# One pool of eight PSUM banks for attention and front, and a new written order of the steps

## The chip, the cores and the metric

The kernel runs on one core of a Trainium2 chip. The core has five engines that run their own instruction queues and meet only at semaphores: TensorE (PE: matmuls; its weight loads are listed as PEld), VectorE (DVE), ScalarE (ACT), GpSimd (POOL) and SyncE (SP, which issues most DMAs). Matmuls write to PSUM, eight banks of 128 partitions x 512 float32; DVE and ACT read the results from there. The metric is the device time of one execution in microseconds (us).

## The reference

The input is x, 8 batches of 512 tokens with 256 features, all in float32. With H = 16 heads of width 16 and a latent width of 32:

```
qkv = x @ c_attn_w.T + c_attn_b                 # q, k, v: 16 heads x 16
q_lat = q @ q2l_w.T + q2l_b; k_lat, v_lat with kv2l
q_lat, k_lat = rope(q_lat), rope(k_lat)         # t*cos + rotate_half(t)*sin
att = softmax(causal((q_lat @ wqk_w.T + wqk_b) @ k_lat.T * 32**-0.5))
y = (att @ v_lat) @ l2o_w.T + l2o_b;  x = layernorm(x + y @ cproj_w.T + cproj_b)
xn = layernorm(x)*g + b                         # as 4 x 1024 tokens
logits = xn @ (layernorm(slot_embeds)).T        # 16 experts x 64 slots
slots = softmax(logits over tokens).T @ xn      # dispatch
eout = (gelu(slots@Wg+bg) * (slots@Wu+bu)) @ Wd + bd    # F = 512, per expert
x = layernorm(x + softmax(logits over slots) @ eout)    # combine
```

The result has to agree with float32, so products that need it are done as three products of split operands (a high part of reduced precision and the rest).

## The kernel before

**Stages.** Setup (0 to 37 us) prepares weights. Attention (to about 558) works on one group of four heads at a time; a batch has four groups, written here as batch.group. The front of the second half (dispatch and the slots) overlaps attention's end and runs to 805; then come the sixteen experts (gate_up and the way down) and combine.

**Steps.** PE's work in attention and front is a list of named steps. In attention, for each group: `lat` (latent q and k), `wqk`, six `max` steps (scores of one shape each, line 1460, with the causal mask added by L1463), `neg` (transposes the negated row maxima, L1468), six `exp` steps (the scores again, transposed, with the maxima folded in, L1476), four `pv` steps (L1487) and `yT` (L1494). Once a batch: `v`, `yTT` (L1500), `cproj` (L1509). In the front, per round: `s1` (logits; split products, L455 to L457), `topT` (L1534), `topB` (L1540), `c2` (transposes of the combine weights, L1563), `sumT` (L1546), `sumB` (L1553), `zT` (L1516), `slots` (L455 to L457).

The other engines have lists of their own. DVE: `max` (reduces a max step, L1170), `negmax` (two instructions, L1178 and L1180), `qlo` (drains wqk's bank and makes the low part of q, L1164), `shuffle` (L1144), `cos` (L1160), `wv` (L1118 to L1121), `v`, `yT`, `ln` (the layernorm), `sel`, `slots` (L1277), `sumT` (L1267), `weight` (splits of expert weights, L1068 and L1071). ACT: `lat` (L817), `khi`, `qhi` (L845, L851), `exp` (drains an exp step with the exponential, L873), `y` (L880), `e` (L943, L944), `c2` (L962), `weight`. POOL: `sin` (L703), `add` (L709), `klo` (L713), `mask` (zeroes the part above the diagonal of the exponentials, L723; `pv` waits for it), `bias` (L729), `lo` (L740), `sum` (L745, L747). SP: `stack` (copies of q and k into the stacked layout that the score matmuls read, L410), `store`, `z`, `c2`, `slots` (L575), `weight` (L513; wg, wu, wd of an expert).

**Order.** Each list is made by `order()` (L55 to L95). A step of attention stands at 32 x batch + 8 x group + an offset in slots from tables such as `PE_AT` and `DVE_AT`; the first steps have places of their own in `PE_EARLY` and the like. The list is sorted by that. The front's steps come from lists for one round (`PE_FRONT`, and `PE_LAST` for the last), and `PE_JOIN` says how many attention steps are left when each of the first front steps comes in.

**PSUM.** `fills()` (L98 to L112) hands out three pairs of banks (`ring`) in turn to every step of `PAIR_STEPS`. The fourth pair (`tail`) is split: one bank, `misc`, for `wqk`, `neg` and `yT`, and one, `ybank`, for `pv`; it becomes a fourth pair behind the last of those. A PE step waits on one semaphore for its pair (or bank) to be drained:

```
    for n, s in enumerate(steps):
        if n == last:
            free.insert(0, RING)
        if s[0] in PAIR_STEPS:
            r = free.pop(0)
            free.append(r)
```

So a step waits for the third last holder of a pair, whichever that was. In a steady group, exp and max steps alternate, and the second `max` step of the next group has the pair of an `exp` step three back.

Of the kernel before, what the change touches and what calls it, by code (L numbers as in the profile page):

```python
# [38 lines left out]
UNIT_SLOTS = GROUP_SLOTS / len(MAX_UNITS)  # L39


PE_AT = {"lat": -20.25, "wqk": -9.25, "max": 0.0, "neg": 11.0, "exp": 13.25, "v": 14.55, "pv": 15.75, "yT": 28.75, "yTT": 53.5, "cproj": 58.5, "wv": -10.384, "seT": 5.624}
ACT_AT = {"stack": -9.0, "xth": -30.5, "lat": -22.0, "khi": -12.85, "qhi": -9.6, "neg": 9.57, "exp": 11.74, "y": 22.25, "yTT": 52.85, "apply": 76.25, "wlat": -30.402, "senorm": -2.024, "seT": 7, "seh": 9.429}
DVE_AT = {"xtl": -32.0, "blat": -28.9, "kvrows": -28.8, "slotg": -28.781, "shuffle": -21.3, "cos": -17.25, "qlo": -10.0, "max": -3.11, "negmax": 6.05, "v": 11.5, "yT": 26.15, "cproj": 55.1, "ln": 56.75, "wlat": -30.314, "wv": -17.071, "sestat": -23.24, "sescale": -7.5, "sel": 9.985}
POOL_AT = {"sin": -26.06, "add": -23.69, "klo": -21.92, "mask": 2.69, "bias": 42.5}
SP_AT = {"xt": -52.5, "x": 28.5, "stack": -22.15, "store": 83.25}

PE_EARLY = {("lat", 0, 1): -11.099, ("lat", 0, 2): -6.473, ("lat", 0, 3): 2.93, ("wqk", 0, 0): -9.817, ("wqk", 0, 1): -5.784, ("wqk", 0, 2): 5.42, ("v", 0): 14.309}
ACT_EARLY = {("lat", 0, 1): -17.39, ("lat", 0, 2): -6.025, ("lat", 0, 3): 2.059, ("khi", 0, 0): -14.377, ("khi", 0, 1): -5.841, ("khi", 0, 2): 5.453, ("qhi", 0, 0): -13.3, ("qhi", 0, 1): -4.402, ("qhi", 0, 2): 4.692, ("xth", 1): 1.5, ("stack", 0, 0): -6.105}
# [8 lines left out]

# [1640 lines left out]
```

## Time and profile before

| what | us |
|---|---|
| three runs | 1200.65, 1199.85, 1196.84; median 1199.85 |
| profiled execution | 1196.4, its span 1194.7 |
| busy in the span | PE 1140.9 (96%), DVE 780.1, ACT 662.9, POOL 579.2 |
| TensorE clock granted | 0.986 of full speed |

The span is the time from the first to the last instruction of the profiled execution. A busy share is the time in which an engine worked on something; PE's includes modelled ends of its pipelined matmuls, so that short pauses between them are not seen in it. The shares are means over stages that differ much, so the rows below are mostly of single stretches.

### The profile page before, as it was taken

The numbers are of one execution on the slowest core, as the hardware profiler recorded it, in microseconds if no ns is written. First come the engines' busy times: TensorE is split into PE (matmuls) and PEld (weight loads), VectorE is DVE, ScalarE is ACT, GpSimd is POOL, SyncE is SP. The second block draws the span as 40 slices with busy tenths as digits, with TensorE's granted clock in tenths as the row PEclk, the third lists the DMA queues.
The fourth block names the chain that finished last, engine by engine and source line by source line (L and its number), as shares of the span: only waits on it lengthen the run. The fifth ranks groups of instructions, "written<-read, shape, count | busy, mean of one in ns | idle before, by whom it ended". The sixth has DMA issues, their size and how long they took to land.

```text
span 1194.7 us, 19111 instructions
## 1 busy us (share of the span) xinstructions
PE 1140.9 (96%) x6849; PEld 897.2 (75%) x6882; DVE 780.1 (65%) x1251; ACT 662.9 (55%) x946; POOL 579.2 (48%) x399
## 2 busy tenths in 40 slices
PE   7799999999999999988999999979999999999996
PEld 5566667676666666656788888858888888888885
DVE  6878787979797978766677777644455454523344
ACT  2555466565656565656797777755555555530112
POOL 5555555555555556522666666664444544430000
PEclk9899999999999999999899999999999999999998
DMA  5645544645565454631144335365555445365661
GB/s 152 143 106 130 123 115 103 159 113 152 125 155 131 115 157 92 180 98 54 40 160 161 125 125 186 108 195 185 166 183 184 140 157 165 114 216 166 244 224 53
DMA packets 126670, 170.29 MB, mean 143 GB/s; under 512 B 47041, under 2 KB 77186, under 8 KB 126594
## 3 DMA queue, kind: packets, MB, share of 16 engines
q1 hardware_dynamic: 124018, 167.95, 48.2%
q10 hardware_dynamic: 2576, 1.35, 0.5%
q8 instruction: 45, 0.74, 0.3%
q14 instruction: 31, 0.25, 0.1%
HBM read 72.26 MB, written 37.75 MB: 92 GB/s over the span
## 4 chain that ended last, share of the span: by engine, by line
PE 79%; ACT 8%; DVE 6%; issue 3%; POOL 1%; ACTq 1%; DMA 1%; SPq 1%; another core or an unknown queue 0%; DVEq 0%; POOLq 0%
PE ring L455 11%; PE ring L456 11%; PE ring L457 11%; PE ring L1626 7%; PE tail L1487 6%; PE ring L1476 5%; PE ring L1460 4%; PE tail L455 4%; PE tail L456 4%; PE tail L457 4%; ACT pt L873 2%; PE ring L1509 2%; PE tail L1626 2%; PE ring L1563 2%; ACT x L892 2%
## 5 line engine op out<-in xcount | busy, mean ns | idle before, releaser
L1170 DVE TENSOR_REDUCE mx<-ring 128x4 f32<-128x512 f32 (+2 forms) x192 | 199.4, 1041 | 71.9 <-PE ring L1463 54.3
L873 ACT ACTIVATE pt<-ring 128x1024 f32<-128x1024 f32 (+1 forms) x192 | 167.4, 882 | 87.3 <-PE ring L1476 87.1
L723 POOL TENSOR_SCALAR_AFFINE_SELECT pt<-pt 128x512 f32<-128x512 f32 x128 | 81.7, 638 | 192.9 <-ACT pt L873 192.9
L1476 PE MATMUL ring<-qks 98*128 98x256 f32 (+3 forms) x512 | 136.7, 370 | 3.9 <-DVE mx L1170 1.9
L1460 PE MATMUL ring<-qks 96*128 96x384 f32 (+3 forms) x512 | 118.7, 334 | 9.0 <-DMA qks<-stg 3.5
L740 POOL TENSOR_TENSOR dl<-e,dh 128x1024 fp32r<-128x1024 f32 x32 | 76.5, 2404 | 93.4 <-ACT e L944 93.4
L764 POOL TENSOR_TENSOR hl<-hid,hh 128x512 fp32r<-128x512 f32 x64 | 82.7, 1302 | 77.1 <-ACT hh L979 77.1
L817 ACT ACTIVATE lat<-ring,blat 128x512 f32<-128x512 f32 x64 | 40.6, 685 | 128.3 <-PE ring L457 117.4
L1476 PEld LDWEIGHTS ring<-qks 98*128 98x128 f32 x512 | 79.0, 190 | 37.0 <-issue 20.1
L1288 DVE SCALAR_TENSOR_TENSOR hid<-ring,bias_e,gate 128x512 f32<-128x512 f32 x64 | 47.8, 747 | 80.9 <-ACT gate L973 47.0
L1460 PEld LDWEIGHTS ring<-qks 96*128 96x128 f32 x512 | 78.5, 192 | 29.5 <-ACT pt L873 18.8
L709 POOL TENSOR_TENSOR rope<-rope,rot 128x1024 f32<-128x1024 f32 x31 | 75.0, 2421 | 35.9 <-DVE rope L1160 35.9
L1626 PE MATMUL ring<-eo,c 128*128 (+1 forms) x384 | 88.3, 379 | 0.0
L1487 PE MATMUL tail<-pt,va 128*32 128x512 f32 (+3 forms) x1024 | 82.8, 439 | 0.4 <-POOL pt L723 0.4
L973 ACT ACTIVATE gate<-ring,bias_e 128x512 f32<-128x512 f32 x64 | 44.1, 689 | 67.3 <-PE ring L457 62.1
L1626 PEld LDWEIGHTS ring<-eo,c 128*128 128x128 f32 x384 | 72.9, 190 | 9.9
L756 POOL TENSOR_TENSOR wul<-wu,wuh 128x1024 fp32r<-128x1024 f32 x16 | 42.4, 2653 | 75.7 <-ACT wuh L798 75.7
L1013 ACT ACTIVATE y<-y,nmr,r 128x256 f32<-128x256 f32 x32 | 16.7, 589 | 104.7 <-DVE nmr L1353 104.7
L703 POOL TENSOR_TENSOR rot<-rot,sin 128x1024 f32<-128x1024 f32 x31 | 73.9, 2383 | 1.0 <-DVE rot L1144 0.9
L979 ACT ACTIVATE hh<-hid 128x512 fp32r<-128x512 f32 x64 | 40.2, 628 | 58.3 <-PE tail L457 49.3
L455 PE MATMUL tail<-wdh,hh 128*128 128x256 f32 x240 | 67.9, 283 | 0.5 <-POOL hl L764 0.5
L457 PE MATMUL tail<-wdl,hh 128*128 128x256 f32 x240 | 67.9, 283 | 0.0
(246 smaller groups left out, 3050.9 us busy)
## 6 DMA issues: line engine op xcount, KB each, us to landing
qks<-stg SPq DMA_DIRECT2D x378, 128.0 KB, 2.4
c_dram<-c2s SPq DMA_DIRECT2D x32, 512.0 KB, 5.0
c<-c_dram SPq DMA_DIRECT2D x32, 512.0 KB, 6.2
sl_dram<-sls SPq DMA_DIRECT2D x32, 256.0 KB, 3.4
wg<-in_wg SPq DMA_DIRECT2D x16, 512.0 KB, 5.3
wu<-in_wu SPq DMA_DIRECT2D x16, 512.0 KB, 6.0
wd<-in_wd SPq DMA_DIRECT2D x16, 512.0 KB, 6.9
sl<-sl_dram SPq DMA_DIRECT2D x16, 512.0 KB, 4.5
```

The source lines that it names most:

```text
L455: nc.tensor.matmul(dst, lh, rh, start=first, stop=False)
L456: nc.tensor.matmul(dst, ll, rh, start=False, stop=False)
L457: return nc.tensor.matmul(dst, lh, rl, start=False, stop=last)
L723: nc.gpsimd.affine_select(out=m, in_=m, compare_op=ALU.is_ge, fill=0.0, base=0, pattern=[[0, GH], [1, P]], channel_multiplier=-1).then_inc ...
L740: nc.gpsimd.tensor_tensor(out=dl[h][:, rows, :], in0=e2[u][:, :, :], in1=fp(dh[h][:, rows, :]), op=ALU.subtract).then_inc(d_low, 1)
L764: nc.gpsimd.tensor_tensor(out=hl[:, f, :], in0=hid[f % 2][:, :], in1=fp(hh[:, f, :]), op=ALU.subtract).then_inc(hid_low, 1)
L873: nc.scalar.activation(pt[j][:, h:h + heads, 0:n], heads_of(tile, heads, n), ACT.Exp, scale=SCALE).then_inc(empty, 1)
L1170: nc.vector.tensor_reduce(out=mx[:, g, h:h + heads, i], in_=heads_of(tile, heads, (i + 1) * P), axis=AX.X, op=ALU.max).then_inc(empty, 1)
L1460: nc.tensor.matmul(scores[:, h, :], qks[0:KS_ROWS, g, 0, h0 + h, i * P:(i + 1) * P], qks[0:KS_ROWS, g, 1, h0 + h, 0:n], start=(h % some == ...
L1476: last = nc.tensor.matmul(scores[:, h, :], qks[0:KS_ROWS + 2, g, 1, h0 + h, j * P:(j + 1) * P], qks[0:KS_ROWS + 2, g, 0, h0 + h, j * P:T], ...
L1487: last = nc.tensor.matmul(ybank[h * L:(h + 1) * L, j * P:T], va[:, j, g * GH + h, :], pt[j][:, h, 0:T - j * P], start=(j == 0), stop=(j == ...
L1626: last = nc.tensor.matmul(acc[i][t // 2][:, t % 2, 0:DO], c2[i][:, n, t * P:(t + 1) * P], eo[:, n, b, :], start=(n == 0), stop=(n == NS - 1))
```

## The change

The tail and the ring become one tensor of eight banks. `width(step)` gives each PE step one or two banks: single ones for `wqk`, `neg`, `yT`, `sumT`, `sumB`, small `max` and `exp` units, and for `pv` one that is held from its first step until `y` has read it. `fills()` gives every step the adjacent banks that an estimate says are free soonest. The estimate is a table, `HOLD`, in steps from a fill to its drain. A step waits for each previous holder of its banks, so for one or two.

```diff
+BANKS = 8
-    free, left = list(range(RING)), [0] * QUAD
+    free, left, holder = [0] * BANKS, [0] * BANKS, [None] * BANKS
     for n, s in enumerate(steps):
-        if s[0] in PAIR_STEPS:
-            r = free.pop(0)
-            free.append(r)
-            slot_of[s], turn_of[s] = r, left[r]
-            left[r] += 1
+        w = width(s)
+        if w:
+            k = min(range(BANKS - w + 1), key=lambda k: max(free[k:k + w]))
+            before[s] = tuple(dict.fromkeys(h for h in holder[k:k + w] if h))
+            slot_of[s], turn_of[s] = k, left[k]
+            left[k] += 1
+            for m in range(k, k + w):
+                free[m], holder[m] = n + HOLD[s[0]], s
+def width(step):
+    name = step[0]
+    if name == "max":
+        i, _, heads = MAX_UNITS[step[3]]
+        return -(-heads // (4 // (i + 1)))
+    if name == "exp":
+        j, _, heads = EXP_UNITS[step[3]]
+        return -(-heads // (4 // (NT - j)))
+    if name == "pv":
+        return 1 if step[3] == 0 else 0
+    return 2 if name in PAIR_STEPS else 1 if name in BANK_STEPS else 0
+PAIR_STEPS = ("lat", "v", "yTT", "cproj", "wv", "seT", "zT", "s1", "topT", "topB", "c2", "slots")
+BANK_STEPS = ("sumT", "sumB", "wqk", "neg", "yT")
+HOLD = {"lat": 2.873, "max": 2.51, "exp": 3.27, "v": 3.885, "yTT": 2.654, "cproj": 3.994, ..., "wqk": 5.032, "neg": 3.484, "yT": 2.965, "pv": 12.433}
             for st in pe_steps:
-                    pe.wait_ge(pair_drained[slot(st)], fill_count(st, 0))
+                    for held in before[st]:
+                        pe.wait_ge(bank_drained[slot(held)], fill_count(held))
-PE_AT = {"lat": -20.25, "wqk": -9.25, "max": 0.0, "neg": 11.0, "exp": 13.25, "v": 14.55, "pv": 15.75, ...}
+PE_AT = {"lat": -20.188, "wqk": -8.805, "max": 0.262, "neg": 11.3, "exp": 13.478, "v": 14.312, "pv": 15.612, ...}
-DVE_AT = {..., "qlo": -10.0, "max": -3.11, ..., "wv": -17.071, ...}
+DVE_AT = {..., "qlo": -10.961, "max": -2.629, ..., "wv": -11.543, ...}
-    ("topT", 0), ("c2", 0, 0), ("sumT", -1, 1), ("topB", 0), ("sumB", -1, 1), ("slots", -1, 1), ("c2", 0, 1), ("slots", 0, 0),
-    ("sumT", 0, 0), ("sumB", 0, 0), ("c2", 0, 2), ("c2", 0, 3), ("slots", 0, 1), ("sumT", 0, 1), ("sumB", 0, 1),
+PE_LAST = (("topT", 0), ("c2", 0, 0), ("sumT", -1, 1), ("topB", 0), ("sumB", -1, 1), ("c2", 0, 1), ("slots", -1, 1), ("slots", 0, 0), ("sumT", 0, 0),
+    ("sumB", 0, 0), ("c2", 0, 2), ("sumT", 0, 1), ("c2", 0, 3), ("slots", 0, 1), ("sumB", 0, 1))
```

All offsets of all engines are new, there are lists of their own for the rounds up to the first (`PE_FIRST` and the like), and batch 7's last steps have places of their own. Most new offsets leave the order as it was. What really moves:

- PE: `wv` between the first two halves of group 0.0's and 0.1's `lat`; `wqk` of 0.2 behind `seT`; the first `s1` before `exp` 7.3.4 (the fifth exp step of group 7.3), the second before `yT` of 7.2; in round 0 `c2` 2 and 3 before `s1` of the next; in later rounds `c2` before `topT`, `sumB` before `topB`; in the last round `sumT` of the last half before the last `c2` and `slots`.
- DVE: `qlo` before the first `max` of the next group, in every group (it was behind it); `wv` behind the first `qlo`; `cos` of 0.2 before the first `max`; small moves in the front.
- ACT: `khi` of 0.2 before `lat` of 0.3, two exps of 7.3 before `y` of 7.2, in round 0 the last `e` behind the second `s1`.
- POOL: `sin` of 0.3 before `klo` of 0.2; `bias` of each batch before a mask and `klo` instead of behind them.
- SP: the wd load of the first expert behind two stores of slots, `store` a little earlier, `c2` stores a little later.

## Rows read from the trace of the kernel before

**Rows 1.** Table of stretches (length; busy PE, PEld, DVE, ACT, POOL; clock, DMA share, GB/s).
```profile
80.00:484.00 404.00, 399.67 (x2697) 274.54 (x2720) 332.75 (x513) 236.74 (x362) 232.27 (x187) 1.00 0.53 131
484.00:570.00 86.00, 73.02 (x514) 51.02 (x515) 56.11 (x106) 53.89 (x79) 26.09 (x27) 0.98 0.34 97
570.00:768.00 198.00, 198.00 (x1098) 170.30 (x1099) 137.88 (x155) 158.36 (x196) 133.81 (x63) 0.99 0.38 129
```

**Rows 2.** List of waits, weight loads of PE (us in total, times, longest us).
```profile
PEld ring L1460 <- ACT pt L873: 18.8, 56, 0.8
```

**Rows 3.** Timeline, group 4.1 (start us, us, engine, line, operation, tiles, idle before and releaser).
```profile
312.26 2.38 POOL L703 TENSOR_TENSOR rot<-rot,sin 128x1024 f32<-128x1024 f32 x1
...
312.60 0.70 PE L1476 MATMUL ring<-qks 98*128 98x384 f32 x2
...
313.45 0.54 PEld L1460 LDWEIGHTS ring<-qks 96*128 96x128 f32 x4 [0.46 <-ACT pt L873]
...
314.60 0.63 POOL L723 TENSOR_SCALAR_AFFINE_SELECT pt<-pt 128x512 f32<-128x512 f32 x1
...
314.70 0.55 DVE L1180 SCALAR_TENSOR_TENSOR negmax<-mx,negmax 128x16 fp32r<-128x16 f32 x1
...
315.40 0.27 PE L1468 MATMUL tail<-ident,negmax 128*32 128x128 f32 x1
```

**Rows 4.** Timeline of DVE in group 7.1.
```profile
500.74 0.74 DVE L1164 SCALAR_TENSOR_TENSOR stg<-tail,bwq,stg 128x512 fp32r<-128x512 f32 x1
...
501.60 0.17 DVE L1180 SCALAR_TENSOR_TENSOR negmax<-mx,negmax 128x16 fp32r<-128x16 f32 x1
```

**Rows 5.** Chain of waits, setup (start us, us, what).
```profile
22.78 0.61 DVE wvh L1118
...
25.56 0.77 DVE stg L1164
...
30.70 5.36 DMA qks<-stg
...
42.44 3.22 POOL rope L709
```

**Rows 6.** Timeline of ACT, setup.
```profile
24.06 0.69 ACT L851 ACTIVATE stg<-tail,bwq 128x512 fp32r<-128x512 f32 x1 [0.56 <-PE tail L1447]
```

**Rows 7.** Timeline, fourth exp and second max step, unblocked.
```profile
64.94 0.61 PE L1476 MATMUL ring<-qks 98*128 98x384 f32 x2
...
65.38 0.68 PE L1460 MATMUL ring<-qks 96*128 96x256 f32 x4
```

**Rows 8.** Timeline, fourth and fifth max step, first a plain group.
```profile
304.41 0.96 DVE L1170 TENSOR_REDUCE mx<-ring 128x2 f32<-128x768 f32 x1 [2.64 <-PE ring L1463]
...
305.37 0.65 PE L1460 MATMUL ring<-qks 96*128 96x512 f32 x2
...
339.76 0.95 DVE L1170 TENSOR_REDUCE mx<-ring 128x2 f32<-128x768 f32 x1
...
340.54 0.65 PE L1460 MATMUL ring<-qks 96*128 96x512 f32 x2
```

**Rows 9.** Timeline of PE, batch 7's last groups.
```profile
512.29 0.63 PE L1460 MATMUL ring<-qks 96*128 96x128 f32 x4 [1.27 <-DMA qks<-stg]
...
535.93 0.74 PE L1476 MATMUL ring<-qks 98*128 98x256 f32 x4 [0.41 <-ACT pt L873]
```

**Rows 10.** Timeline of PE, start of round 1.
```profile
569.97 0.77 PE L455 MATMUL tail<-seh,xnh 128*128 128x512 f32 x1 [3.77 <-DVE xnl L1224]
```

**Rows 11.** Timeline of ACT, a middle round.
```profile
654.48 1.03 ACT L962 ACTIVATE c2s<-ring 128x1024 f32<-128x1024 f32 x1 [0.72 <-PE ring L1563]
```

**Rows 12.** Timelines of POOL and of PE, last round.
```profile
792.28 2.16 POOL L747 TENSOR_TENSOR e<-e 128x512 f32<-128x512 f32 x1
...
792.52 0.48 PE L455 MATMUL ring<-dh,zh 128*128 128x512 f32 x1
...
799.77 0.62 PE L1553 MATMUL ring<-ident,res 128*128 128x128 f32 x4 [1.09 <-DVE res L1267]
```

More of the change, by code:

```diff
@@ L24 @@
 RING = 3
-QUAD = 4
+BANKS = 8
 GROUP_SLOTS = 8
@@ L38 @@
 PV_WITH = (1, 1, 3, 3)
[L39 to L49, printed above, removed]
@@ L52 @@
-SP_EARLY = {("stack", 0, 0): -23.836, ("stack", 0, 1): -10.032, ("stack", 0, 2): -1.655}
-def order(at, front=(), last=(), join=(), early={}):
+MAX_SLOTS = GROUP_SLOTS / len(MAX_UNITS)
+EXP_SLOTS = GROUP_SLOTS / len(EXP_UNITS)
+PE_AT = {"lat": -20.188, "wqk": -8.805, "max": 0.262, "neg": 11.3, "exp": 13.478, "v": 14.312, "pv": 15.612, "yT": 28.859, "yTT": 54.21, "cproj": 58.33, "wv": -17.819, "seT": 6.548}
+ACT_AT = {"stack": -8.881, "xth": -30.982, "lat": -22.407, "khi": -12.522, "qhi": -9.634, "neg": 9.57, "exp": 12.057, "y": 22.089, "yTT": 52.154, "apply": 76.936, "wlat": -29.34, "senorm": -3.495, "seT": 7.217, "seh": 8.071}
@@ L57, in order @@
+POOL_EARLY = {("sin", 0, 0): -22.599, ("sin", 0, 1): -19.495, ("sin", 0, 2): -5.326, ("add", 0, 0): -29.871, ("add", 0, 1): -18.091, ("add", 0, 2): -3.315, ("klo", 0, 0): -20.014, ("klo", 0, 1): -9.385, ("klo", 0, 2): -1.035, ("bias", 7): 251.358}
+SP_EARLY = {("stack", 0, 0): -28.64, ("stack", 0, 1): -27.972, ("stack", 0, 2): -2.796, ("store", 7): 300.253, ("x", 7): 251.351}
+def order(at, front=(), first=(), last=(), join=(), early={}):
     todo = []
@@ L86, in order @@
     for w in range(-2, B):
-        for name, ahead, *more in (last if w == B - 1 else front):
+        for name, ahead, *more in (last if w == B - 1 else first if w <= 0 else front):
             b = ahead if name == "weight" else w + ahead
@@ L153 @@
+PE_JOIN = (21, 10, 6, 3, 1)
+ACT_JOIN = (11, 6, 5, 2, 1, 1, 1, 1, 1, 1, 1, 1, 1, 1, 1, 1, 1, 1, 1, 1, 1, 1, 1, 1, 1, 1, 1, 1, 1, 1, 1, 1, 1, 1, 1, 1, 1)
+DVE_JOIN = (5, 5, 4, 4, 2, 2)
+SP_JOIN = (5, 5, 2, 2, 2, 1, 1, 1, 1, 1, 1, 1, 0, 0)
 POOL_JOIN = ()
-PAIR_STEPS = ("lat", "max", "exp", "v", "yTT", "cproj", "wv", "seT", "zT", "s1", "topT", "topB", "sumT", "sumB", "c2", "slots")
-MISC_STEPS = ("wqk", "neg", "yT")
+PAIR_STEPS = ("lat", "v", "yTT", "cproj", "wv", "seT", "zT", "s1", "topT", "topB", "c2", "slots")
@@ L159, in block_kernel @@
+BANK_STEPS = ("sumT", "sumB", "wqk", "neg", "yT")
+HOLD = {"lat": 2.873, "max": 2.51, "exp": 3.27, "v": 3.885, "yTT": 2.654, "cproj": 3.994, "wv": 4.216, "seT": 6.603, "zT": 4.129, "s1": 4.661, "topT": 4.644, "topB": 3.4, "sumT": 3.087, "sumB": 2.219, "c2": 3.06, "slots": 2.88, "wqk": 5.032, "neg": 3.484, "yT": 2.965, "pv": 12.433}
 def block_kernel(nc, a, out):
```

318 lines of the change are left out of this document (159 added, 159 removed).

## The prediction, made before the change was run

> **What bounds the kernel now.** I read the table of stretches first [rows 1]: TensorE (PE) is busy 399.67 of the 404 us of steady attention, 73.02 of 86 where attention runs out and the front starts, and all of 198.00 in the front's rounds; only setup, hand-over and last round leave it openly idle. But a busy PE hides short stalls, because the ends of matmuls are modelled. The list of waits shows them on the weight loads: those of the max step (L1460) waited 18.8 us, 56 times, for ACT's exp [rows 2]. The timelines of one group then show which wait is real.
>
> One group of attention (312 to 316 us, [rows 3]) has two. The second max step starts at 313.45 after its weight load idled 0.46 for exp's drain of its bank pair. The transpose of the negated maxima (neg, L1468) starts at 315.40, and the DVE instruction that makes its input (L1180) ended at 314.70 + 0.55 = 315.25. That gap, 0.15, stands in 24 of the 32 groups. In the other eight (groups 1.2 to 6.2, as batch.group, where cproj stands ahead of neg, and 7.1 and 7.2) neg comes 0.9 to 4.3 after its input and PE is the bound.
>
> What holds L1180? POOL. It ends at 315.25, and POOL's mask at 314.60 + 0.63 = 315.23; it takes 0.55 there, and 0.17 with no POOL work beside it [rows 4]. In all steady groups it ends 0.02 to 0.03 after the mask, and the mask follows POOL's sin product (312.26 + 2.38 = 314.64) without a pause. So POOL's chain sets neg, from the exp unit that releases the mask ahead of sin, and PE time saved in between is given back in front of neg. The Trainium skill, "SBUF — State Buffer", "Who interferes with whom", says that a VectorE instruction with two SBUF inputs and a GpSimd instruction that reads SBUF exclude each other for a whole instruction; the trace agrees to 0.03 us. Without that rule L1180 would take 0.17, neg would come up to 0.38 sooner, PE would be the bound, and (1) below would be kept in every group, which is R1's sum.
>
> **The change part by part**, against the profiled run (span 1194.7, run 1196.4; the median of the three runs shown is 1199.85, 3.45 higher, and I add that at the end).
>
> *A, setup: -1.3.* The chain there goes through DVE: the wv instructions (from 22.78) stand ahead of the shuffle and qlo (25.56), and qlo releases the stack copies on which PE waits until 30.70 + 5.36 [rows 5]. Now wv follows qlo of group 0, and qlo starts behind qhi on ACT, which ends at 24.06 + 0.69 = 24.75 [rows 6]: 0.75 earlier. wqk of group 2 waits for POOL's add (42.44 + 3.22 = 45.66); with cos ahead of the first max reductions and the seT transposes in front of wqk that wait is covered, but then DVE's max reductions bind, so I take only 0.55 for it. POOL's klo of group 2 goes behind sin and its stack copy with it; PE reads that copy well after: 0. Bounds: -0.3 to -2.0.
>
> *B, steady attention: +2.8.* The matmul order inside a group stays. Three things move. (1) The second max step takes banks whose holder is drained some 0.8 earlier, so its wait goes: the distance from the exp step at 312.60 is 0.85 [rows 3], while unblocked it is 0.44 (64.94 to 65.38, [rows 7]); of the 0.41 some 0.1 is a mask matmul that stays, so it is worth 0.31. By the POOL chain above it is kept only where neg isn't POOL's: 6 + 2 groups, 8 x 0.31 = -2.5. (2) The fifth max step now takes the banks of the fourth, three steps back, where it had those of the last exp. It starts 0.14 after ACT's drain of those (305.23), at 305.37. The fourth's reduction by DVE ends at 304.41 + 0.96 = 305.37 and would give 305.50, 0.13 later; in the group whose DVE also does the layernorm it ends at 339.76 + 0.95 = 340.71 against a start at 340.54, 0.31 later [rows 8]. No POOL chain spans this part. Batches 1 to 6 pay 0.13 three times and 0.31 once or a little more (0.73), 4.4 in all, four groups at the ends 0.9 more: +5.3. Bounds: 0, if the bank were free in time, to +5.3. (3) qlo moves ahead of the next group's first max reduction, in a stretch where DVE then waits for POOL anyway: 0, and SP's stack copies behind it have slack in steady state. Bias on POOL (2.40) goes in front of a mask into an idle 1.87; the pv behind that mask comes later still: 0. 115 steps now wait for two banks. A second wait that is already met shows in no row; the nearest is the 0.14 from drain to start, and 12 of the fifth max steps could pay it twice, 1.7. PE's queue runs ahead of the matmuls, and I take 0. Ends for B: -6.5 (both stalls really go, no new one) to +7.0.
>
> *C, 484 to 558: -1.6.* Batch 7's stack copies go out 0.4 earlier (qlo starts at 500.74 behind a max reduction that it now goes ahead of; of its 0.6 I take two thirds), and PE waits 1.27 for them at 512.29. s1 of round 0 moves in front of the exp step that idled 0.41 at 535.93 [rows 4, 9], and fills some 1.1 of that and later pauses; 0.1 comes from one more bank. The layernorm and the last yT stay as they are. Bounds 0 to -2.6.
>
> *D, 558 to 590: -0.8.* s1 waits 3.77 for DVE at 569.97 [rows 10]. Two c2 steps (some 1.7) move into that hole, but e moves behind s1 on ACT and delays the sums by POOL by about 1. Bounds 0 to -1.7.
>
> *E, front's rounds: +0.9.* The slots step now takes the banks of the c2 step that ACT drains at 654.48 + 1.03 = 655.51, when PE reaches slots [rows 11]; with the 0.14 from drain to start, six or seven rounds pay it. PE is full there, so nothing else can be won. Bounds 0 to +1.2.
>
> *F, last round: +1.5.* sumT of the last half moves in front of the last c2 and slots. It needs POOL's sum, which ends at 792.28 + 2.16 = 794.44, while PE had c2 done and slots started at 792.52 [rows 12]. Slots now start after 794.44 and the twelve transposes of sumT and c2, at 0.1 each: 795.67, 3.15 later. In exchange sumB follows slots at once, where now sumT (0.60) and a wait of 1.09 stand between: 1.69 back, 1.46 left. What follows (ACT, DVE, the first gate_up) shifts as it is. The wd load goes behind two slots stores on SP, some 16 us later; its split on ACT and DVE fits behind the 3 us hole there: 0. Bounds +0.5 (POOL's sum comes sooner by what C and D win) to +3.
>
> Sum: -1.3 + 2.8 - 1.6 - 0.8 + 0.9 + 1.5 = +1.5, so 1197.9 against 1196.4, and 1201.3 at the level of the median.
>
> **The rivals.**
> R1, faster: POOL's chain gives way with PE, for instance because the mask reads an exp that comes sooner. Then every group keeps 0.31: 30 x -0.31 + 5.3 = -4.0 in place of +2.8, total -5.3, 1194.5. For it speaks that POOL is busy only 232.27 of 404 [rows 1], so a mask that starts sooner meets a free engine; against it the 0.02 to 0.03 between POOL and DVE, and that sin starts without a pause behind the mask [rows 3].
> R2, nothing in steady state: banks come free in time for the fifth max step as well and the 0.31 goes back to neg. B is 0 and the sum -1.3: 1198.5. For it: DVE is busy only 332.75 of 404 [rows 1]. Against it: 305.37, DVE's end and PE's start in one [rows 8].
> R3, slower: steps of the front take banks whose readers (ACT, DVE) are the late side. Place: 536 to 805. Each of some four switches a round costs 0.14 to 0.3, about 0.6 a round for eight rounds in place of E's 0.9, C and D gain nothing but C's 0.3, and F costs 3: -1.3 + 2.8 - 0.3 + 4.8 + 3 = +9.0; with half of the switches +6.6, which I take: 1206.4. It decides once a reader ends later than 0.14 before the step that takes its bank, and slots against c2 is already there.
> R4, slower: the clock. Between 80 and 484 it was granted at 1.00, between 484 and 570 at 0.98 [rows 1]. Should new bank waits bring steady attention to 0.98, 2% of 404 is 8, on top of the forecast 1209.4. The Trainium skill, "TensorE: Matmul & The Clock Gate", "A second HAM failure mode: psum-queue depth-cycling", describes a kernel that lost clock by cycling through PSUM banks; the trace here cycles through four pairs at 1.00.
>
> **How the numbers follow.** Chances: forecast 0.35 (its own range 1198.3 to 1204.3), R1 0.30, R2 0.15, R3 0.17, R4 0.03. A measurement of this kernel can tell about 0.3% from no change, so the bounds are 1196.25 and 1203.45. Faster: 0.27 of R1, 0.04 of R2, 0.01 of the forecast, 0.32. Slower: 0.15 of R3, R4's 0.03, 0.07 of the forecast: 0.25. The same: 0.43. The range takes in R1 with 1.5 of spread and R3: 1193 to 1206.5.
>
> **What would show it.** In the profile after: neg still 0.15 after L1180 and L1180 still 0.03 after POOL's mask, with the distance from the exp step to the second max step at 0.54 instead of 0.85 (B1); the fifth max step's weight load idle for DVE L1170 in 28 groups (B2); the first max step after 36.19 some 0.7 earlier (A); the wait for the stack copies at 512 shorter by 0.4 and s1 before 536.5 (C); gate_up's first matmul some 1.3 later relative to the round (F). Neg of group 4.1, now at 315.40, would come at 315.40 - 1.3 + 1.4 (half of B) = 315.5; if it comes over 1.5 sooner, B has the wrong sign and R1 is nearer.

## The result and the profile after

The changed kernel is slower by 0.4%: 1203.64 us (median) against 1198.85, ratio 1.0039, 95% interval 1.0026 to 1.0052. One run of the eight at 1872 us, a disturbed one, is left out. The forecast was 1201.3, with a range of 1193 to 1206.5.

The time was hit better than its working deserved. The sum of the parts was +1.5 on the profiled execution, and the profiled execution after is 1204.4, +8.0. I had then added 3.45 us because the profiled run of before lay that far under its median. The run of after lies 0.8 above its own median. Between the medians the difference is 4.8.

The table of stretches, answering to [rows 1] (same columns):

```profile
80.00:484.00 404.00, 394.97 (x2701) 273.30 (x2700) 334.72 (x509) 237.27 (x361) 231.31 (x185) 1.00 0.54 132
484.00:570.00 86.00, 75.54 (x537) 53.87 (x535) 56.34 (x107) 53.24 (x78) 27.75 (x28) 0.98 0.30 86
570.00:768.00 198.00, 194.07 (x1079) 166.53 (x1080) 139.79 (x158) 157.32 (x193) 128.76 (x61) 0.99 0.41 133
```

PE's busy time in steady attention falls from 399.67 to 394.97, yet the stretch needs only 2 us more. Most of the "lost" busy time is no new pause: it stood in front of the second max step, largely under the modelled end of the exp matmuls, and now stands in front of neg, where it can be seen. The granted clock is the same, so R4 (the clock in steady attention) is out.

The waits of PE and of its weight loads (engine, line, awaited engine, tile and line: us in total, times, longest), answering to [rows 2]:

```profile
PE psum L1487 <- DVE negmax L1199: 10.3, 22, 1.2
PE psum L1565 <- POOL e L762: 5.0, 2, 4.0
...
PEld psum L1479 <- DVE mx L1189: 8.6, 22, 0.9
```

The waits of the max step (now L1479) for ACT's exp, 18.8 us in 56 places, are down to 3.3 us in 7. In their place stand waits of neg (L1487) for the second negmax instruction (L1199, once L1180) and of the max step for DVE's reduction.

Group 4.1 after, answering to [rows 3]:

```profile
315.23 2.38 POOL L718 TENSOR_TENSOR rot<-rot,sin 128x1024 f32<-128x1024 f32 x1
...
315.58 0.70 PE L1495 MATMUL psum<-qks 98*128 98x384 f32 x2
...
316.12 0.63 PE L1479 MATMUL psum<-qks 96*128 96x256 f32 x4
...
317.56 0.64 POOL L738 TENSOR_SCALAR_AFFINE_SELECT pt<-pt 128x512 f32<-128x512 f32 x1
...
317.65 0.29 PE L1482 MATMUL psum<-maskb,identb 128*128 128x128 bf16 x2
...
317.68 0.55 DVE L1199 SCALAR_TENSOR_TENSOR negmax<-mx,negmax 128x16 fp32r<-128x16 f32 x1
...
318.37 0.27 PE L1487 MATMUL psum<-ident,negmax 128*32 128x128 f32 x1 [0.43 <-DVE negmax L1199]
```

The matmuls just before neg stood here in the kernel before:

```profile
315.10 0.29 PE L1463 MATMUL ring<-maskb,identb 128*128 128x128 bf16 x2
```

Exp to second max step is now 316.12 - 315.58 = 0.54, as predicted, instead of 0.85 (in half of the groups it was 0.78 before). Until the last matmuls before neg PE has saved 0.43: 317.65 - 315.58 = 2.07 instead of 315.10 - 312.60 = 2.50. From there on nothing is won: POOL's mask ends at 318.20, L1199 at 318.23, 0.03 later, and neg starts 0.14 after that. From the start of the sin product to the start of neg it is 3.14 us in both kernels (315.40 - 312.26; 318.37 - 315.23). The 0.43 that PE saved has become PE's wait of 0.43.

The fourth and fifth max step, answering to [rows 8]; the first three rows are a plain group, the last two the group whose DVE also does the layernorm:

```profile
307.24 0.96 DVE L1189 TENSOR_REDUCE mx<-psum 128x2 f32<-128x768 f32 x1 [2.83 <-PE psum L1482]
...
307.63 0.73 PE L1495 MATMUL psum<-qks 98*128 98x512 f32 x2
...
308.25 0.73 PE L1479 MATMUL psum<-qks 96*128 96x512 f32 x2
...
342.36 0.95 DVE L1189 TENSOR_REDUCE mx<-psum 128x2 f32<-128x768 f32 x1
...
343.37 0.73 PE L1479 MATMUL psum<-qks 96*128 96x512 f32 x2
```

The fifth max step starts 0.05 or 0.06 after DVE is through (307.24 + 0.96 = 308.20; 342.36 + 0.95 = 343.31). Before, its weight load also started 0.05 after ACT's drain (305.23), and the matmul, at 305.37, 0.57 behind the exp step:

```profile
304.80 0.73 PE L1476 MATMUL ring<-qks 98*128 98x512 f32 x2
...
305.28 0.30 PEld L1460 LDWEIGHTS ring<-qks 96*128 96x128 f32 x2 [0.19 <-ACT pt L873]
```

That distance is 0.57 in all steady groups of the kernel before, and the shortest that any kernel shows from batch 1 on is 0.54, in batch 7. So of the 0.14 from the drain to the matmul at most 0.03 was waiting; the rest was PE's work on the exp step.

**Where the 8.0 us arose**, by the start of the same named step in the two profiled runs:

| stretch | predicted | measured |
|---|---|---|
| A, setup, to neg 0.2 (81.33 before) | -1.3 | +1.6 |
| B, to neg 7.0 (487.81) | +2.8 | +2.0 |
| C, to topT 0 (557.93) | -1.6 | +1.3 |
| D, to slots 0.0 (585.26) | -0.8 | -1.9 |
| E, to slots 7.0 (781.60) | +0.9 | +2.8 |
| F, to the first gate_up (804.14) | +1.5 | +3.1 |
| experts and combine | 0 | -0.9 |

### The profile page after: what moved, and what is told of

Read it like the earlier page. It is cut to its first block, busy times and chain, and to the rows that moved or that the text cites. A ratio compares the mean times of both kernels' runs of the same rounds, so it can differ in the third digit from the quotient of the medians.

```text
span 1202.7 us, 19268 instructions
## 1 busy us (share of the span) xinstructions
PE 1142.5 (95%) x6882; PEld 903.3 (75%) x6882; DVE 786.3 (65%) x1251; ACT 664.5 (55%) x946; POOL 576.2 (48%) x399
## 3 DMA queue, kind: packets, MB, share of 16 engines
q10 hardware_dynamic: 2576, 1.35, 0.5%
## 4 chain that ended last, share of the span: by engine, by line
PE 71%; DVE 14%; ACT 6%; issue 5%; POOL 3%; DMA 1%; SPq 1%; ACTq 0%; DVEq 0%; POOLq 0%
PE psum L470 14%; PE psum L471 14%; PE psum L472 14%; PE psum L1647 9%; PE psum L1505 5%; PE psum L1495 4%; DVE mx L1189 4%; PE psum L1479 3%; PE psum L1582 2%; ACT stg L866 2%; DVE negmax L1197 1%; ACT ys L896 1%; DVE negmax L1199 1%; ACT pt L888 1%; POOL dl L755 1%
## 5 line engine op out<-in xcount | busy, mean ns | idle before, releaser
L1189 DVE TENSOR_REDUCE mx<-psum 128x4 f32<-128x512 f32 (+2 forms) x192 | 199.4, 1040 | 63.7 <-PE psum L1482 63.6
L888 ACT ACTIVATE pt<-psum 128x1024 f32<-128x1024 f32 (+1 forms) x192 | 167.5, 881 | 77.8 <-PE psum L1495 77.2
L1495 PE MATMUL psum<-qks 98*128 98x256 f32 (+3 forms) x512 | 137.8, 372 | 5.2 <-DVE ytok L1212 2.4
L1479 PE MATMUL psum<-qks 96*128 96x384 f32 (+3 forms) x512 | 118.6, 334 | 5.6 <-DMA qks<-stg 3.9
L1647 PE MATMUL psum<-eo,c 128*128 128x256 f32 (+1 forms) x512 | 110.8, 379 | 0.0
L1495 PEld LDWEIGHTS psum<-qks 98*128 98x128 f32 x512 | 80.5, 191 | 37.9 <-issue 24.3
L1647 PEld LDWEIGHTS psum<-eo,c 128*128 128x128 f32 x512 | 97.2, 190 | 13.2
L1479 PEld LDWEIGHTS psum<-qks 96*128 96x128 f32 x512 | 79.1, 193 | 23.5 <-DVE mx L1189 8.6
L1505 PE MATMUL psum<-pt,va 128*32 128x512 f32 (+3 forms) x1024 | 82.2, 439 | 0.0
L470 PE MATMUL psum<-wdh,hh 128*128 128x256 f32 x256 | 72.7, 284 | 0.5 <-POOL hl L779 0.5
```

The lines of the kernel that those rows point to most:

```text
L470: nc.tensor.matmul(dst, lh, rh, start=first, stop=False)
L888: nc.scalar.activation(pt[j][:, h:h + heads, 0:n], heads_of(tile, heads, n), ACT.Exp, scale=SCALE).then_inc(empty, 1)
L1189: nc.vector.tensor_reduce(out=mx[:, g, h:h + heads, i], in_=heads_of(tile, heads, (i + 1) * P), axis=AX.X, op=ALU.max).then_inc(empty, 1)
L1479: nc.tensor.matmul(scores[:, h, :], qks[0:KS_ROWS, g, 0, h0 + h, i * P:(i + 1) * P], qks[0:KS_ROWS, g, 1, h0 + h, 0:n], start=(h % some == ...
L1495: last = nc.tensor.matmul(scores[:, h, :], qks[0:KS_ROWS + 2, g, 1, h0 + h, j * P:(j + 1) * P], qks[0:KS_ROWS + 2, g, 0, h0 + h, j * P:T], ...
L1505: last = nc.tensor.matmul(tile_of(sums)[h * L:(h + 1) * L, 0, j * P:T], va[:, j, g * GH + h, :], pt[j][:, h, 0:T - j * P], start=(j == 0), ...
```

## The experiments

All were timed over five rounds beside the kernel before. Ratios are to before, with their 95% interval. "Attention steady" below is the change from neg 0.2 to neg 7.0 against the kernel before, some 6.4 batches.

**1 and 2. The two halves of the change alone.** The theory (POOL's chain binds neg, the new banks cost at the fifth max step) against the rivals that the order or the banks alone carry the loss.

```diff
 alloc_only: the pool, width() and HOLD of the change; all tables and lists as before
-PE_AT = {"lat": -20.188, "wqk": -8.805, "max": 0.262, ...}
+PE_AT = {"lat": -20.25, "wqk": -9.25, "max": 0.0, ...}
 order_only: all tables and lists of the change; banks handed out in turn as before
-            k = min(range(BANKS - w + 1), key=lambda k: max(free[k:k + w]))
+            if s[0] in ("wqk", "neg", "yT", "pv"):
+                k, w = 7 if s[0] == "pv" else 6, 1
+            else:
+                k, w = free.pop(0), 2
+                free.append(k)
```

> The step order of before, with the pool of eight banks and its allocation as in the changed kernel. Theory (POOL's chain sets neg, the pool's new holders cost): between neg of 0.2 and neg of 7.0 attention takes 1.5 to 2.5 us longer than before (the changed kernel took 2.0 longer there), L1199 ends 0.03 after POOL's mask as it does in both kernels, and setup shows no loss (within 0.5 at neg of 0.1). Time 1200 to 1203. Rival (the new order is what costs, the pool by itself gains the 0.31 per group): steady attention 5 or more us shorter, time about 1194.

> The new orders on all engines, with banks handed out as before (three pairs in turn, one bank for wqk, neg and yT, one for pv). Theory: steady attention as before within 0.5 us (qlo's move gives and costs nothing), neg of 0.0 late by 0.56 because POOL's klo stands behind sin there, gate_up late by 3 in the last round; the wait for ytok of 2.4 at the exp steps of group 7.3 is gone, since those banks don't meet any more. Time 1199 to 1203. Rival (the allocation is what costs): time as before, 1198.9 within 1.

alloc_only: 1207.61, 1.0078 (1.0058 to 1.0097). Attention steady +1.5, at the lower end of what was expected, but setup +2.5 (no loss was expected there), batch 7 up to neg 7.3 +3.4 and the rounds, slots 0.0 to slots 7.0, +3.3; the whole is above the expected span. In setup 1.6 of it stand between the first max step and neg 0.0, where max steps wait 0.87 and 1.71 for DVE's reductions: with the old order the pool costs there too. order_only: 1227.49, 1.0234 (1.0210 to 1.0259), far outside what was expected. Attention steady is 0.0 (+4.25 at neg 0.2, +4.21 at neg 7.0), so qlo's move costs nothing there, as predicted. The loss is in the front, about 3.2 us a round (+5.9 at slots 0.0, +28.0 at slots 7.0). Its waits:

```profile
PE psum L477 <- ACT c L950: 14.7, 8, 2.9
PE psum L477 <- DVE sll L1091: 6.4, 1, 6.4
```

In each round a split product (L477) waits for ACT to have read an earlier pair. An order of the front written for one way of handing out banks doesn't fit another. Each half alone is worse than both together (0.78% and 2.34% against 0.39%), so the effects of the two edits don't add up.

**3 and 4. Does L1178 wait for POOL because it has two SBUF inputs?** The first negmax instruction with one input, in the kernel before and in the one after:

```diff
-nc.vector.scalar_tensor_tensor(out=negmax..., in0=mx..., scalar=-1.0, in1=zeros..., op0=ALU.mult, op1=ALU.add)
+nc.vector.tensor_scalar(out=negmax..., in0=mx..., scalar1=-1.0, scalar2=None, op0=ALU.mult)
```

> The kernel before, with L1178 as a tensor_scalar (mx times -1) that has one input in SBUF instead of two. Theory (a DVE instruction with two SBUF inputs waits until a POOL instruction is over): L1178 takes 0.17 beside POOL's sin, L1180 gets in front of POOL's mask and ends about 0.4 earlier, neg is then bound by PE, 0.15 earlier in 24 groups: 3 to 3.6 us less, about 1195.5. Rival (the coincidence with POOL is one of time only, or the new form waits as well): L1180 ends 0.03 after the mask as now, no change.

> The changed kernel with the same edit. Theory: PE idles 0.43 in front of neg in 21 groups, of which 0.38 goes: 8 to 9 us less than the changed kernel, about 1195, so that the 0.31 that the pool gives at the second max step is kept in every group and shows in the time. Rival as above: 1203.6, no change.

1197.35, 1.0000 (0.9986 to 1.0014), and 1203.36, 1.0041 (1.0025 to 1.0057): nothing changed, and the expected gains of 3 and 8 us didn't come. Group 4.1 of before with one input:

```profile
311.71 2.38 POOL L703 TENSOR_TENSOR rot<-rot,sin 128x1024 f32<-128x1024 f32 x1
...
313.71 0.41 DVE L1178 TENSOR_SCALAR negmax<-mx 128x16 fp32r<-128x16 f32 x1
314.05 0.63 POOL L723 TENSOR_SCALAR_AFFINE_SELECT pt<-pt 128x512 f32<-128x512 f32 x1
...
314.16 0.55 DVE L1179 SCALAR_TENSOR_TENSOR negmax<-mx,negmax 128x16 fp32r<-128x16 f32 x1
```

The instruction with one SBUF input still ends with the sin product (314.12 against 314.09), so this form doesn't undo the waiting, and the second instruction waits out the mask in any case.

**5 and 6. Take the mask away from beside negmax.** The mask whose place is between the two negmax instructions waits, in all batches but the last, until the second is done. Nothing else is changed, so this tells whether POOL's chain binds neg.

```diff
             elif name == "mask":
 ...
+                if j == 1 and b < B - 1:
+                    pool.wait_ge(neg_ready, group(b, g) + 1)
```

> The kernel before, in which POOL's mask of the second key tile waits for negmax of the next group (one wait more on POOL, nothing left out). The one-input form of L1178 waited for POOL like the old one, so this takes POOL's mask out of the way instead. Theory (POOL's chain of sin and mask sets neg): L1180 follows L1178 at once, ends 0.38 earlier, neg becomes PE's own, 0.15 earlier in 24 groups: -3.4, about 1194.8. Rival (DVE is late by itself): no change, 1198, or slower because pv waits for the mask.

> The changed kernel with the same edit. Theory: of the 0.43 that PE idles in front of neg 0.38 goes in 21 groups: -8, about 1195.5; distances between negs of neighbouring batches fall from 63.40 to about 62.2. Rival: no change, 1203.5.

before_mask: 1193.63, 0.9956 (0.9939 to 0.9973). after_mask: 1194.99, 0.9966 (0.9950 to 0.9982), 8.65 below the changed kernel. Group 4.1 of after_mask:

```profile
311.68 2.38 POOL L718 TENSOR_TENSOR rot<-rot,sin 128x1024 f32<-128x1024 f32 x1
...
313.41 0.68 DVE L1199 SCALAR_TENSOR_TENSOR negmax<-mx,zeros 128x16 fp32r<-128x16 f32 x1
...
314.13 0.17 DVE L1201 SCALAR_TENSOR_TENSOR negmax<-mx,negmax 128x16 fp32r<-128x16 f32 x1
...
314.45 0.27 PE L1489 MATMUL psum<-ident,negmax 128*32 128x128 f32 x1
314.46 0.63 POOL L740 TENSOR_SCALAR_AFFINE_SELECT pt<-pt 128x512 f32<-128x512 f32 x1 [0.40 <-DVE negmax L1201]
```

The second negmax instruction takes 0.17 in place of 0.55, and sin's start to neg 2.77 in place of 3.14. A mask delayed by 0.40 makes the kernel faster. It isn't free: pv's weight loads now wait for it, at most 0.35 in 20 steady groups and 6.9 us in all,

```profile
315.15 0.13 PEld L1507 LDWEIGHTS psum<-pt,va 128*32 128x32 f32 x4 [0.35 <-POOL pt L740]
```

but steady attention is 7.2 shorter than in the changed kernel all the same. Attention steady is -3.7 in before_mask and -5.2 in after_mask, so with the lock gone the new banks are worth 1.5 us there, where with the lock they cost 2.0. The gain of the change was there, and POOL took it back. The fifth max step's cost stays in after_mask (0.62 to 0.90 behind the exp step).

**7 and 8. Banks by what the trace showed.** The estimate in counted steps is replaced by a written list of first banks, chosen from the fills and drains in the profile of the changed kernel; after_placed_mask has the mask's wait as well.

```diff
-            k = min(range(BANKS - w + 1), key=lambda k: max(free[k:k + w]))
+            k = int(PLACED[len(slot_of)])
```

> The changed kernel with the orders kept and every step's banks taken from a list that was chosen from the fills and drains in its own profile, so that no step takes a bank whose reader ends within 0.14 before it. Theory (the choice by counted steps costs, not the pool): the fifth max step starts 0.5 to 0.6 after the exp step in front of it in every group instead of 0.62 to 0.89, -0.6 per batch, -4 in all; the wait for ytok in group 7.3 goes, -2.4 and what the clock lost behind it; c2 of round 2 -0.9, slots -0.1 a round. Sum -8, about 1195.5. Rival (the order is the cost, or the saved time goes back into neg): within 2 of 1203.6.

> Both edits on the changed kernel. Theory: they act in different parts of a group (neg to the second exp step, second exp step to neg), so they add up: -16, about 1187.5. Rival (one takes what the other gives): no less than 1194.

1197.81, 1.0000 (0.9988 to 1.0013), and 1189.44, 0.9923 (0.9897 to 0.9949). The first is 5.8 below the changed kernel, not 8, and the second 14.2 below it, not 16. The fifth max step stands 0.57 behind the exp step again in all steady groups, as expected. Attention steady is -2.7 in after_placed (against +2.0) and -10.4 in after_placed_mask; the two edits alone gain 4.7 and 7.2 there on the changed kernel and both together 12.3, so they add up. The wait for ytok in group 7.3 stayed, 2.36: the list was laid out from a profile that already contained it, so the banks looked no worse there than others. A measured time is not a time at which something could have been done.

**9. The two ends.** klo of group 0.2 goes back ahead of sin of 0.3, and the five lists of the last round are those of before.

```diff
-POOL_EARLY = {..., ("klo", 0, 2): -1.035, ...}
+POOL_EARLY = {..., ("klo", 0, 2): -2.5, ...}
-PE_LAST = (..., ("sumT", 0, 0), ("sumB", 0, 0), ("c2", 0, 2), ("sumT", 0, 1), ("c2", 0, 3), ("slots", 0, 1), ("sumB", 0, 1))
+PE_LAST = (..., ("sumT", 0, 0), ("sumB", 0, 0), ("c2", 0, 2), ("c2", 0, 3), ("slots", 0, 1), ("sumT", 0, 1), ("sumB", 0, 1))
```

> The changed kernel with two places of its order as before, far apart: in setup POOL's klo of group 0.2 ahead of sin of 0.3, and in the last round the five lists (PE, ACT, DVE, POOL, SP) as before. Theory: in setup L1199 no longer waits 1.19 beside klo, neg of 0.0 comes 0.56 earlier, PE's idle time there falls under a microsecond, the clock stays up for the next lat and neg of 0.1 is 2 earlier; in the last round gate_up comes 3.1 earlier counted from slots of 7.0. Sum about -5, 1198.5. Rival for setup (the clock fell for another reason, wv or lat's new places): neg of 0.0 gains 0.56 and neg of 0.1 no more than that. Rival for the last round (the slots step waits for its bank, not for sumT): gate_up within 1 of the changed kernel.

1199.94, 1.0012 (0.9997 to 1.0026). The last round is 3.9 us shorter (slots 7.0 to gate_up -0.8 against before, where the change had +3.1), 3.1 were expected. The whole is 3.7 below the changed kernel, 5 were expected. In setup the wait of neg 0.0 is gone (0.23 in place of 1.24) and neg 0.0 to neg 0.1 takes 15.39 in place of 16.74 (before: 15.12). In absolute time neg 0.0 didn't come earlier (52.82), but this execution was late from the start: its first max step stood at 37.47, not at 36.00. From there to neg 0.0 it is 15.35, in the changed kernel 16.77 and before 16.03.

**10. The middle.** bias of batch 7 goes back behind the masks, yT of 7.1 on DVE ahead of the layernorm's xn, and in round 0 the last e on ACT ahead of the second s1.

```diff
-POOL_EARLY = {..., ("bias", 7): 251.358}
+POOL_EARLY = {..., ("bias", 7): 300}
-DVE_JOIN = (5, 5, 4, 4, 2, 2)
+DVE_JOIN = (5, 4, 4, 4, 2, 2)
-    ("c2", 0, 3), ("s1", 1, 1), ("e", 0, 3), ("sumB", 0, 0), ("s1", 1, 2), ("s1", 1, 3))
+    ("c2", 0, 3), ("e", 0, 3), ("s1", 1, 1), ("sumB", 0, 0), ("s1", 1, 2), ("s1", 1, 3))
```

> The changed kernel with three moves taken back: POOL's bias of batch 7 behind the masks, DVE's xn of round 0 behind yT of 7.1 (both as before), and ACT's e 3 of round 0 ahead of the second s1. The banks stay. Theory: the wait for ytok at the exp step of 7.3 (2.42) goes, because DVE's xnl no longer stands 3.15 beside POOL's bias ahead of it, and the half clock behind it: cproj of 7 comes 2.5 to 4 earlier; slots of round 0 doesn't wait 1.1 for POOL. Sum about -4.5, 1199. Rival (the bank is the cause and takes the wait wherever DVE stands): under 1 us.

1200.36, 1.0013 (1.0000 to 1.0026). neg 7.3 to topT 0 takes 1.3 less than before, where the change took 2.3 more: the three edits are worth 3.5 there. slots 0.0 to 0.1 is +0.25 instead of +1.16. The wait at c2 stayed. The whole is 3.3 below the changed kernel, 4.5 were expected.

**11 and 12. All of it, and the same with the old order.** final has the changes of 6, 9 and 10 and a list of banks laid out anew; old_order_placed_mask has the tables and lists of before with pool, list and mask's wait.

```diff
 final
+                if j == 1 and b < B - 1:
+                    pool.wait_ge(neg_ready, group(b, g) + 1)
+            k = int(PLACED[len(slot_of)])
 old_order_placed_mask: the same two, PE_AT and all other tables and lists as in the kernel before
```

> All of it: the changed kernel with mask behind negmax, banks from the list (made anew from the profile of the kernel with both edits), and the moves of the two kernels above taken back. If the parts add up: 1189.4 - 5 - 4.5 = 1180. If the list of banks solved part of the middle already: 1184. Steady attention 61.2 to 61.5 per batch against 63.10 before.

> The step order of before on all engines, the pool of eight banks with a list of banks chosen from a profile of that order, and the mask behind negmax. Theory (the pool and the lock decide, the new order contributes little): steady attention 61.4 to 61.6 per batch against 63.10 before, front and last round as before, 1185 to 1187. Rival (the new order carries a good part of what the kernel called final gains): 1190 or more. Rival on the other side: 1181, the order contributes nothing.

final: 1180.53, 0.9853 (0.9832 to 0.9874), better than both kernels, by 23.1 us than the changed one, and what the parts add up to. The first seven rows of its list of waits on PE hold no neg, and in steady attention PE's busy time is

```profile
80.00:484.00 404.00, 402.51 (x2801) 282.22 (x2795) 337.80 (x521) 242.62 (x373) 245.57 (x193) 1.00 0.55 136
```

402.51 of 404: in steady attention next to nothing is left of the pauses that show on PE. That PE alone bounds it now isn't shown, since its busy time hides short waits; the largest one left on its weight loads that names another engine is pv's for POOL's mask:

```profile
PEld psum L1524 <- POOL pt L757: 8.7, 25, 0.5
```

old_order_placed_mask: 1187.96, 0.9926 (0.9908 to 0.9944), between the expected 1185 to 1187 and the rival's 1190. So half of the gain (0.74% of 1.47%) needs none of the new order, and most of that half (0.44%) not even the pool, as before_mask shows. The new order, once its bad moves are taken back, is worth the other half by the medians, 7.4 us, if it is the order: final's list of banks was the second one, made anew from the trace of a kernel that already had a list, the old order's was chosen from a profile of that order which isn't named. No run separates list and order. The profiled runs show less, 4.3 (1181.28 against 1185.60, the lowest run of that kernel), of which 3.3 stand at the first gate_up (-14.1 against -10.8). Some 0.9 more is hidden in the start: final's first max step stood at 36.26 in its profiled execution, the other's at 35.36. The rest of the difference between 4.3 and 7.4 is not explained. In steady attention the two differ by 0.4 only; 2.6 arise between neg 7.0 and topT 0.

## Why the prediction was right or wrong

**A, setup: wrong (-1.3 predicted, +1.6).** The "0.75 earlier" itself held as a distance: from the first shuffle to qlo it is 5.95 instead of 6.68 (19.16 to 25.11, 18.88 to 25.56). Of it 0.26 was lost behind qlo, where the stack copies are (qlo to the first max step takes 10.89 instead of 10.63). Another 0.28 went because the first shuffle came later, which says little: its date varies by 1.1 among four kernels whose setup is the same. So the first max step stands at 36.00 instead of 36.19. The 0.55 for wqk of group 2 didn't come: the first negmax instruction starts 15.20 behind the first max step, before it was 14.82 (after_ends: 14.78). The step that failed is "PE reads that copy well after: 0" for klo, and for a reason that isn't the copy. The timeline of the changed kernel at 51 us:

```profile
51.33 1.26 POOL L728 TENSOR_TENSOR stg<-rope,stg 128x512 fp32r<-128x512 f32 x1
51.44 1.19 DVE L1199 SCALAR_TENSOR_TENSOR negmax<-mx,negmax 128x16 fp32r<-128x16 f32 x1
...
52.77 0.27 PE L1487 MATMUL psum<-ident,negmax 128*32 128x128 f32 x1 [1.24 <-DVE negmax L1199]
...
53.81 0.79 PE L470 MATMUL psum<-xth,wlath 128*128 128x512 f32 x1 [0.77 <-DVE mx L1189]
...
54.41 0.63 PE L471 MATMUL psum<-xth,wlatl 128*128 128x512 f32 x1
```

klo, behind sin now, stands beside the negmax instruction, which takes 1.19 instead of 0.17; PE idles 1.24 and then 0.77, and the lat matmuls that follow come every 0.43 instead of every 0.23. The same stretch in the table of stretches, after and before:

```profile
53.00:60.00 7.00, 6.23 (x18) 4.72 (x18) 6.62 (x5) 1.49 (x4) 2.36 (x1) 0.52 0.74 173
```

```profile
53.00:60.00 7.00, 6.71 (x43) 5.42 (x42) 6.37 (x6) 2.82 (x4) 3.82 (x2) 1.00 0.72 166
```

The part of klo is shown by after_ends: without that neighbour neg 0.0 stands 15.35 behind the first max step, 1.1 to 1.4 less than in four kernels with it, and neg 0.1 1.35 closer to neg 0.0. But the second wait, 0.77, is the lat step's for banks that DVE's reduction drains, so it belongs to the pool. It stays in after_ends (0.78), and the clock there is 0.79 from 52 to 60, against 0.57 in the changed kernel. In after_placed, whose list gives lat other banks, it is gone: klo's 1.24 is still there, yet the clock is 0.84 from 52 to 60 and neg 0.0 to 0.1 takes 14.44, less than before. So klo's wait and the bank's wait cost 0.3 or nothing there one by one, and 1.6 where both stand; my sum had neither.

The dates in setup need care: neg 0.0 stood at +0.56, +1.68, +1.69 and -0.34 in four kernels whose setup is the same. That spread arises ahead of the first max step (the first lat matmul starts between 11.58 and 14.18 in them); from the first max step to neg 0.0 they take 16.42 to 16.77, against 16.03 before. Counted so, A is -0.2 to the first max step, +0.7 to neg 0.0, +1.6 to neg 0.1 and -0.5 to neg 0.2.

**B, steady attention: right, size a little off (+2.8 predicted, +2.0).** Every part of the mechanism shows: 0.54 for 0.85 (1), the reduction of DVE as the new releaser (2), no cost of qlo and bias (3, and order_only, steady 0.0), neg 0.03 + 0.14 behind POOL. Only the date of neg 4.1 was missed, 318.37 for 315.5, and that is A: B's share up to there was forecast as 1.4 and was 1.3 (+1.64 at neg 0.2, +2.98 at neg 4.1). Over batches 1 to 6 it is 0.3 a batch, not 0.42. The mis-sized term is the 0.13. It added 0.14 to DVE's end, as if that were the time from a drain to the matmul; that time is 0.05, and the 0.14 before was mostly PE's own work. So the distance from exp to the fifth max step grew from 0.57 to 0.62 in the plain group shown and by 0.05 to 0.15 in others; 0.31 was right for the layernorm's group (0.26 to 0.32). Over neg 0.2 to neg 7.0 this growth adds up to 3.5. Against it stand the six groups where PE is the bound at neg: each is 0.37 to 0.45 shorter, 2.5 together, with the 0.31 and what PE gained behind it. The last 1.0 is spread over the other groups and not assigned. R1 (POOL gives way with PE) is refuted as it stood. after_mask shows its direction right once POOL's mask is out of the way, but not its size: against before_mask the new banks are worth 1.5 us in steady attention, not the 4.0 of R1's sum.

**C: wrong (-1.6 predicted, +1.3).** The predicted gain came: the wait for the stack copies at [rows 9] fell from 1.27 to 0.33 and neg 7.2 stood 1.4 better than neg 7.0. It was lost in one place:

```profile
535.16 2.37 POOL L744 TENSOR_TENSOR x<-x,cpb 128x1024 f32<-128x1024 f32 x1
...
535.47 3.15 DVE L1246 TENSOR_TENSOR xnl<-xn,xnh 128x1024 fp32r<-128x1024 f32 x1 [2.38 <-ACT xnh L916]
...
538.82 0.42 DVE L1212 TENSOR_TENSOR ytok<-psum,sums_r 128x256 f32<-128x256 f32 x1
...
539.39 0.94 PE L1495 MATMUL psum<-qks 98*128 98x384 f32 x4 [2.42 <-DVE ytok L1212]
```

Three parts of the change meet. POOL's bias is moved beside DVE's xnl, which takes 3.15 for its 1.22. DVE's drain of yT (ytok) is put behind the layernorm, so it comes at 538.82, where it was at 532.97. And the pool has given the third exp step of 7.3 a pair of which one bank holds that yT, of group 7.1. In the ring, yT had the bank `misc`, and no exp step could wait for it. The sentence that failed is "the layernorm and the last yT stay as they are"; and "0.1 comes from one more bank" counted the pool's gain and not that it ties steps together that had nothing to do with each other. Behind this wait the s1 products ran at the lower clock for 4 us,

```profile
541.00:545.00 4.00, 4.00 (x14) 3.15 (x12) 0.30 (x1) 1.96 (x3) 0.63 (x1) 0.57 0.00 0
```

granted 0.57, and took 4.34 instead of 2.94, 1.4 more. In after_mask, where the same wait (2.40) was followed by the full clock, neg 7.3 to topT 0 is +0.7 instead of +2.3. after_middle gives 3.5 of it back. The halves show that bank and order are both needed: alloc_only gives the step that yT's bank too, order_only has bias beside xnl (3.16) and the late drain, and in neither does the exp step wait for ytok. Bias and the late drain weren't taken back one by one. This is R3's mechanism (a reader later than the step that takes its bank), in single places and not in every round.

**D: right in sign, -1.9 for -0.8.** The two c2 steps filled the hole; e behind s1 cost nothing here, where I took 1 (D is -1.9 in after_middle as well, with e back in front), and 0.9 in E.

**E, rounds: mis-sized (+0.9 predicted, +2.8).** The slots step against c2 cost little: from slots 1.1 to slots 7.0 it is +0.5 in six rounds, not 0.14 each. The rest is two single waits. In round 0, slots wait for POOL's low part behind the late e (+1.2, of which after_middle gives 0.9 back). In round 2, where PE already was ahead:

```profile
623.95 4.04 ACT L908 ACTIVATE x<-x,nmean,ny 128x256 f32<-128x256 f32 x8
627.90 1.00 ACT L978 ACTIVATE c2s<-psum 128x1024 f32<-128x1024 f32 x1
```

```profile
628.95 1.09 PE L1582 MATMUL psum<-ident,c 128*128 128x128 f32 x8 [0.94 <-ACT c2s L978]
```

The second c2 step takes the banks of the first, which ACT drains only behind eight applies of the layernorm (L908), +1.2. I had looked at a middle round and multiplied; the loss lies in the rounds that aren't like the middle one. In after_placed, whose list avoids that pair, slots 0.1 to 1.1 is +0.7 and not +1.2.

**F, last round: mechanism right, size off (+1.5 predicted, +3.1).** sumT waits for POOL's sum as said:

```profile
800.27 0.93 PE L1565 MATMUL psum<-ident,e 128*128 128x128 f32 x4 [4.04 <-POOL e L762]
800.99 1.91 PE L1582 MATMUL psum<-ident,c 128*128 128x128 f32 x8
802.56 0.78 PE L470 MATMUL psum<-dh,zh 128*128 128x512 f32 x1
```

The slots step starts 4.2 later, counted from slots 7.0, not 3.15, and 1.1 comes back behind it, not 1.69. What was missing is the price of the 4.04 itself: the eight transposes after it took 1.57 instead of 0.85 and the slots step 6.18 instead of 5.56, 1.3 more, because the clock had fallen. Before, that slowness fell on the first gate_up matmuls (the first six of them give back 0.87, which is most of the -0.9 in the experts). after_ends gives 3.9 back.

Of the chances, "slower" had 0.25 and happened, just beyond the bound (0.39% against 0.3%, and the interval reaches below it); "the same" had 0.43. More would have stood on slower if klo, bias, yT and e, each moved to stand beside or behind long work of another kind, had not been priced at 0 or near it.

## What to carry to other kernels

When a short VectorE instruction ends a few hundredths after a GpSimd one in group after group, GpSimd sets that time, however idle it is on the whole; price every move of a GpSimd instruction by what it comes to stand beside, and try a later start of it before rearranging TensorE's order. Sharing PSUM banks in one pool made the second max step's wait shorter here and joined steps that were independent: go through each step's previous holders at the ends of the program, where engines' orders are irregular, before trusting a mean per step. And count with each new wait of TensorE of more than about a microsecond that the matmuls behind it may run at the lower clock, 1.3 to 1.4 us each in two places here.
